# The border between two layers: weights laid out transposed, low parts moved to GpSimd, the first tile quantised earlier

## The reference

```
# layer 0: attention with context, 32 query heads, 8 kv heads, rotary, then a quantised gated FFN
x = x + tanh(g_xattn[0]) * (softmax(rope(LN(x) @ wq) @ rope(ctx @ wk).T / sqrt(128) + mask) @ (ctx @ wv)) @ wo
h = silu(q8(LN(x)) @ q4(Wg).T) * (q8(LN(x)) @ q4(Wu).T)        # q8: rows to 8 bits, q4: weights to 4 bits
x = x + tanh(g_ffn[0]) * (q8(h) @ q4(Wd).T)
# layer 1: attention over the channel axis, per sequence; then a linear layer with routed low-rank parts
q = Wq @ ctx' + bq ; k = Wk @ ctx' + bk ; v = Wv @ LN(x)' + bv  # Wq, Wk, Wv are 64x64, ctx' is [64, 512]
x = x + tanh(g_xattn[1]) * (v @ softmax(q.T @ k).T)
alpha = softmax(router_W[active] @ LN(x) + router_b[active] + log(domain_prior[active]))
x = x + tanh(g_ffn[1]) * (LN(x) @ W_base.T + b_base + 2 * sum_e alpha_e * (LN(x) @ A_e.T) @ B_e.T)
```

## Time and profile before

| | |
|---|---|
| time, median of 3 runs (lowest to highest) | 795.31 us (793.71 to 796.48) |
| the profiled execution | 795.32 us, span from first to last instruction 793.5 us |
| TensorE busy | 780.8 us, 98% of the span, 4940 instructions |
| TensorE weight loads | 638.8 us, 81% |
| VectorE busy | 541.4 us, 68% |
| ScalarE busy | 437.7 us, 55% |
| GpSimd busy | 498.0 us, 63% |
| granted TensorE clock | 1.000 in all slices |
| DMA | 71.02 MB in 77778 packets, 51552 of them under 512 B |

### The profile page before, as it was taken

How to read it: one execution, slowest core, us unless ns; L and a number is a source line. 1 busy time by engine, 2 the same in 40 slices (tenths; PEclk the granted TensorE clock), 3 DMA queues, 4 the chain that set the end, 5 groups by cost and what they waited for, 6 DMA issues and landing times.

```text
span 793.5 us, 13550 instructions
## 1 busy us (share of the span) xinstructions
PE 780.8 (98%) x4940; PEld 638.8 (81%) x4957; DVE 541.4 (68%) x1043; ACT 437.7 (55%) x824; POOL 498.0 (63%) x430
## 2 busy tenths in 40 slices
PE   8999999999999999999999999999999999999998
PEld 7888888888888888888888888888765777777776
DVE  6857866666676545466655555555899987998874
ACT  5754455444454434444454433333579898888773
POOL 2797477645556764475676456546457885887753
PEclk9999999999999999999999999999999999999999
DMA  9312533432523131952113111267273413213101
GB/s 335 107 66 68 139 80 81 133 97 72 148 77 89 40 102 58 47 147 77 63 40 105 43 51 27 36 64 277 82 191 95 107 48 81 74 49 80 48 16 40
DMA packets 77778, 71.02 MB, mean 89 GB/s; under 512 B 51552, under 2 KB 52800, under 8 KB 77328
## 3 DMA queue, kind: packets, MB, share of 16 engines
q1 hardware_dynamic: 77424, 69.82, 34.1%
q10 hardware_dynamic: 288, 0.33, 0.1%
HBM read 49.04 MB, written 6.34 MB: 70 GB/s over the span
## 4 chain that ended last, share of the span: by engine, by line
PE 87%; DVE 4%; DMA 4%; POOL 2%; ACT 2%; issue 1%; another core or an unknown queue 1%; SPq 0%; DVEq 0%
PE bank L81 11%; PE bank L83 10%; PE bank L82 10%; PE bank L554 7%; PE bank L577 6%; PE bank L572 6%; PE bank L573 6%; PE bank L667 4%; PE bank L1645 4%; PE bank L1631 3%; PE bank L1597 2%; PE bank L1568 2%; PE bank L1576 2%; PE bank L1621 2%; DMA w_out<-w_quant 2%; PE bank L1622 2%
## 5 line engine op out<-in xcount | busy, mean ns | idle before, releaser
L970 DVE SCALAR_TENSOR_TENSOR x_res<-bank,gate,x_res 128x512 f32<-128x512 f32 x128 | 95.4, 747 | 74.0 <-PE bank L577 73.4
L1231 POOL TENSOR_TENSOR prob<-prob,row_inv 128x512 f32<-128x512 f32 x32 | 33.4, 1044 | 166.1 <-DVE row_inv L966 159.5
L1217 POOL TENSOR_TENSOR rope_swap<-rope_swap,trig 128x512 f32<-128x512 f32 x80 | 104.0, 1300 | 30.6 <-ACT rope_swap L737 30.3
L736 ACT COPY rope_swap<-bank 64x512 f32<-64x512 f32 x80 | 46.7, 584 | 110.3 <-DVE rope_cos L941 110.2
L941 DVE TENSOR_TENSOR rope_cos<-bank,trig 128x512 f32<-128x512 f32 x80 | 54.2, 678 | 76.5 <-PE bank L83 71.4
L572 PE MATMUL bank<-wo_hi,oT_hi 128*128 128x512 f32 x256 | 101.7, 397 | 1.2 <-DVE x_res L970 0.6
L81 PE MATMUL bank<-xnT_hi,wq_hi 128*128 128x512 f32 x252 | 101.5, 403 | 0.0
L573 PE MATMUL bank<-wo_lo,oT_hi 128*128 128x512 f32 x256 | 100.8, 394 | 0.0
L83 PE MATMUL bank<-xnT_hi,wq_lo 128*128 128x512 f32 x252 | 99.9, 396 | 0.0
L82 PE MATMUL bank<-xnT_lo,wq_hi 128*128 128x512 f32 x252 | 99.5, 395 | 0.0
L1223 POOL TENSOR_TENSOR q_rope<-rope_cos,rope_swap 128x512 f32<-128x512 f32 x64 | 84.2, 1315 | 5.0
(11 more groups left out here) (273 smaller groups left out, 1936.2 us busy)
## 6 DMA issues: line engine op xcount, KB each, us to landing
wq_raw<-in_wq_tiles SPq DMA_DIRECT2D x16, 512.0 KB, 3.8
wo_raw<-in_L_xattn_wo SPq DMA_DIRECT2D x16, 512.0 KB, 3.9
xn<-in_L_ffn_Wd SPq DMA_DIRECT2D x16, 256.0 KB, 3.6
b_ctx<-in_ctx SPq DMA_DIRECT2D x32, 128.0 KB, 2.6
b_k_twice<-b_qk_hi SPq DMA_DIRECT2D x32, 128.0 KB, 2.4
w_T_dram<-w_out SPq DMA_DIRECT2D x28, 128.0 KB, 3.1
w_T<-w_T_dram SPq DMA_DIRECT2D x2, 1376.0 KB, 19.9
xn<-in_L_ffn_Wg SPq DMA_DIRECT2D x10, 256.0 KB, 3.0
```

Of the source, the lines that this page charges most:

```text
L970: dve.scalar_tensor_tensor(out=K.x[:, t, :], in0=wo_ps[t % 2][:, :], scalar=K.gate[:, 0:1], in1=K.x[:, t, :], op0=ALU.mult, op1=ALU.add).t ...
L1217: pool.tensor_tensor(out=sw, in0=sw, in1=sin_b, op=ALU.mult).then_inc(s_rope, 1)
```

## The change

The host lays out W_base, [Wq Wk], Wv (block diagonal) and lora_B transposed, as four more inputs, and the kernel loads them so. `qkv_T`, `base_T`, `b_T` and `bT_copy` are gone: ScalarE casts the high parts from SBUF, and the low parts of W_base are taken by GpSimd instead of VectorE. The first projections move from behind the last output product's tile 0 into slot 30, and write to the banks `proj` instead of `av`. `low_T` moves to slot 31 and writes to `score`; its last product is `logit_T` of its own. `gated_rows` moves from slot 31 to slot 29 on VectorE. GpSimd's iotas and clearing of `qk_w_lo` move into slot 29, its low parts of the context and its clearing of `k_lo` into slot 30. On VectorE `first_front` now comes ahead of the sum of tile 0 of the last unit. In TensorE's second list tiles 1 and 2 of the output product come ahead of `x_transpose(0)`, and `logits(0, 0)` and `low_b_select` ahead of `gate_mm(0, 0)`. SP waits for the last attention product instead of the clearings. Some buffers change places (`qk_lo` with `result`, `k_lo` with `q_stack`), which adds the wait of `first_lo_qk` on `s_w_lo`.

```diff
             sp.wait_ge(M.s_k_zero, 4)
+            sp.wait_ge(s_av, 2 * NPAIR)
...
-            def qkv_T():
-                pe.wait_ge(s_proj_read, len(ALL))
-                pe.wait_ge(R1.s_in, 16 * R1.n_loads)
-                for i in range(3):
-                    mm = pe.transpose(proj[0][0:S, i * S:(i + 1) * S], R1.qkv[i][:, :], K.ident[0:S, 0:S])
-                mm.then_inc(s_w_ps, 1)
...
-            def base_T(c):
-                if c == 1:
...
-                for o in range(DC):
-                    mm = pe.transpose(base_ps[c][:, o * P:(o + 1) * P], R1.base[:, o, c * P:(c + 1) * P], K.ident[:, :])
-                mm.then_inc(s_w_ps, 1)
...
             def low_T(cs):
...
-                    pe.wait_ge(s_sel, 11)
+                    pe.wait_ge(s_sel, 9)
+                    pe.wait_ge(s_soft, 5 * (2 * NPAIR - 1) + 1)
...
-                pe.matmul(trans[:, HD:HD + E_ACT], M.spread[:, :], M.sel_e[:, :], start=True, stop=True).then_inc(s_w_lowT, 1)
...
-            def b_T():
...
-                for c in range(DC):
-                    mm = pe.transpose(proj[0][:, c * P:(c + 1) * P], R1.b[:, c, :], K.ident[:, :])
...
+            def logit_T():
+                pe.wait_ge(s_sel, 11)
+                pe.matmul(score[:, HD:HD + E_ACT], M.spread[:, :], M.sel_e[:, :], start=True, stop=True).then_inc(s_w_lowT, 1)
...
             def low_b_select():
-                pe.wait_ge(s_w_lo, 4)
-                pe.wait_ge(s_w_bT_sb, 1)
-                pe.matmul(proj[1][:, :], M.sel[:, :, :].rearrange("p a n -> p (a n)"), M.bT[:, :], start=True, stop=True
+                pe.wait_ge(M.s_qk_lo[1], 1)
...
             def first_qk(par):
...
-                    pe.wait_ge(s_w_qkv, 4)
+                    pe.wait_ge(s_w_qkv, 1)
...
-                    pe.wait_ge(s_oT_lo, 2 * 2 * NPAIR)
+                    pe.wait_ge(s_proj_read, len(ALL))
...
                 if U == 2 * NPAIR - 1:
-                    base_T(1)
-                    base_T(2)
...
                 if U == 2 * NPAIR - 2:
-                    qkv_T()
-                    base_T(0)
+                    first_qk(0)
+                    first_qk(1)
+                if U == 2 * NPAIR - 1:
+                    low_T((2, 3))
...
             run_slots(slot)
-            base_T(3)
...
             def qkv_weights():
...
+                act.wait_ge(R1.s_in, 16 * R1.n_loads)
+                act.wait_ge(s_zero, 3)
+                act.copy(M.qk_w_hi[:, :], R1.qk[:, :]).then_inc(s_w_qkv, 1)
+                act.copy(M.v_w[:, :], R1.v[:, :]).then_inc(s_w_qkv, 1)
...
             def base_high_part(c):
-                act.wait_ge(s_w_ps, W_BASE + c)
...
+                part = BASE_ORDER[c]
+                act.copy(M.base_hi[:, part, :], R1.base[:, part, :]).then_inc(s_w_hi, 1)
...
-                    if U == 2 * NPAIR - 1:
+                    if U == 2 * NPAIR - 2:
+                        first_split_hi(1)
                         base_high_part(1)
+                        base_high_part(2)
...
+                    if U == 2 * NPAIR - 3:
+                        qkv_weights()
+                        first_split_hi(0)
+                        base_high_part(0)
                     if U == 2 * NPAIR - 2:
-                        qkv_weights()
-                        base_high_part(0)
-                        first_split_hi(0)
-                        first_split_hi(1)
+                        first_hi_qk(0)
+                        first_hi_qk(1)
+                        base_high_part(3)
                         prior_logarithm()
...
+            low_part()
...
             def first_lo_qk(par):
                 dve.wait_ge(M.s_qk_hi[par], 1)
...
+                dve.wait_ge(s_w_lo, par + 1)
...
             def gated_rows():
                 dve.wait_ge(K.s_gate, 1)
+                dve.wait_ge(R1.s_in, 16 * R1.n_loads)
                 dve.tensor_scalar(K.W1.base_row[:, :], K.W1.base_row[:, :], K.gate[:, 3:4], None, ALU.mult).then_inc(M.s_w_logit, 1)
                 dve.tensor_tensor(out=K.W1.bv[:, :], in0=K.W1.bv[:, :], in1=K.gate[:, 1:2], op=ALU.mult).then_inc(M.s_w_logit, 1)
...
                     selection_matrices()
+                    qk_w_low_part()
                 if U < 2 * NPAIR - 1:
                     soft_first(U + 1)
                 else:
                     statistics_end()
-                    base_low_part(1)
-                    gated_rows()
+                    first_lo_qk(0)
                     router_offset()
                 dve.wait_ge(s_oT_hi, 2 * U + 2)
...
                     soft_sum(U + 1)
-                if U == 2 * NPAIR - 2:
-                    qk_w_low_part()
-                    base_low_part(0)
+                if U == 2 * NPAIR - 3:
+                    gated_rows()
...
-            base_low_part(2)
             last = UT * (2 * NPAIR - 1)
...
                 front_tile(dve, M, 0)
+                accumulate(last, UT)
...
+                pool.wait_ge(s_w_hi, c + 1)
+                part = BASE_ORDER[c]
+                pool.tensor_tensor(out=M.base_lo[:, part, :], in0=R1.base[:, part, :], in1=f32(M.base_hi[:, part, :]), op=ALU.subtract
+                                   ).then_inc(s_w_lo, 1)
...
-                        pool.memset(M.v_w[:, :], 0.0).then_inc(s_zero, 1)
+                        pool.wait_ge(s_rope, 2 * rope_of(HKV - 1, len(ITEMS[-1])))
+                        pool.wait_ge(s_sel, 9)
+                        first_split_lo(0)
+                        first_split_lo(1)
+                        pool.wait_ge(M.s_ctx_lo[1], 1)
+                        base_low_part(0)
+                        pool.wait_ge(s_score, 2 * NPAIR)
+                        for i in range(2):
+                            for par in range(2):
+                                pool.memset(f32(M.k_lo[i][par][:, :]), 0.0).then_inc(M.s_k_zero, 1)
                     if U < 2 * NPAIR - 1:
                         normalise(U + 1)
                     for k, (G, pos) in enumerate(items):
...
                             wo_piece(2 * g + jp + 1, u)
+                        if U == 2 * NPAIR - 3 and k == 0:
+                            pool.wait_ge(s_wo_lo[1], NQP * (NPAIR // 2))
+                            pool.iota(M.rank_i[:, :], pattern=[[1, RANK]], base=0, channel_multiplier=0).then_inc(s_zero, 1)
+                            pool.iota(M.part_i[:, :], pattern=[[0, 1]], base=0, channel_multiplier=1).then_inc(s_zero, 1)
+                            pool.memset(f32(M.qk_w_lo[:, :]), 0.0).then_inc(s_zero, 1)
...
+            for c in range(1, DC):
+                base_low_part(c)
             pool.wait_ge(s_x_stat, 2 * UT + 1)
             pool.tensor_tensor(out=K.rstd[:, 0:UT], in0=K.var_eps[:, 0:UT], in1=K.minus_half[:, 0:UT], op=ALU.pow
                                ).then_inc(s_x_stat, 1)
...
         load(W.bv[h * S:(h + 1) * S, :], a["L1_xattn_bv"].unsqueeze(1))
-    for c in range(DC):
-        load(R.b[:, c, :].rearrange("p (e r) -> p e r", e=E_ALL),
-             a["L1_ffn_lora_B"][:, c * P:(c + 1) * P, :].rearrange("e p r -> p e r"))
-    for i, name in enumerate(("L1_xattn_Wq", "L1_xattn_Wk", "L1_xattn_Wv")):
-        load(R.qkv[i][:, :], a[name])
+    load(R.b[:, :], a["lora_b_T"])
+    load(R.qk[:, :], a["qk_T"])
+    load(R.v[:, :], a["v_T"])
...
 def load_base(sp, R, a):
-    sp.dma_start(R.base[:, :, :], a["L1_ffn_W_base"].rearrange("(c p) h -> p c h", p=P)).then_inc(R.s_in, 16)
+    sp.dma_start(R.base[:, :, :], a["base_T"]).then_inc(R.s_in, 16)
...
-    M.qk_lo, M.result = two("b_qk_lo", [P, D], F32R), two("b_result", [P, D])
+    M.result, M.qk_lo = two("b_result", [P, D]), two("b_qk_lo", [P, D], F32R)
...
-    M.q_stack, M.k_lo, M.k_twice = ([two(f"b_{n}{i}", [P, D], F32R) for i in range(2)] for n in ("q_stack", "k_lo", "k_twice"))
+    M.k_lo, M.q_stack, M.k_twice = ([two(f"b_{n}{i}", [P, D], F32R) for i in range(2)] for n in ("k_lo", "q_stack", "k_twice"))
...
                 if t == 0:
-                    pe.wait_ge(L0.s_w_lo, 3)
+                    pe.wait_ge(M.s_w_low, 1)
...
                 pe.matmul(sum_ps(t)[:, :], zT[:, :], low_b[:, :], start=False, stop=True).then_inc(s_y, 1)
-            first.qk(0)
-            first.qk(1)
-            first.low_T((0, 1))
+            first.logit_T()
             first.output(2 * NPAIR - 1, 1)
+            first.output(2 * NPAIR - 1, 2)
             x_transpose(0)
-            first.output(2 * NPAIR - 1, 2)
-            pe.wait_ge(s_qk_lo[0], 1)
+            logits(0, 0)
+            first.low_b_select()
             gate_mm(0, 0)
-            pe.wait_ge(s_qk_lo[1], 1)
             up_mm(0, 0)
-            first.low_b_select()
             pe.wait_ge(s_xT_sb, 1)
             qk(1, 0)
             first.output(2 * NPAIR - 1, 3)
-            logits(0, 0)
             pe.wait_ge(s_gate, 1)
             gate_mm(0, 1)
...
             pe.wait_ge(s_gate, 2)
             gate_mm(0, 2)
-            first.low_T((2, 3))
             logits(0, 3)
```

(4 more changed lines are left out.)

115 lines of the change are left out of this document (38 added, 77 removed).

## The result

Over 22 executions of each on the same chip the changed kernel takes 797.77 us (median; 795.45 to 802.67) and the kernel before 795.27 us (793.58 to 797.45): a ratio of 1.0032, interval 1.0022 to 1.0043, so slower by about 0.3%. The forecast was 795.8 us in a range up to 797.6 us, so the median lies 0.17 us outside. The profiled execution took 798.41 us. Of the 22 executions, four ran at a mean granted clock of 1.000 and took 795.45, 795.66, 796.5 and 797.25 us; the other eighteen ran at 0.993 to 0.998 and took 796.99 us or more (median 797.95).

The account below looks back on a forecast made before the run. TensorE, busy 780.8 of 793.5 us, was taken as the bound, with VectorE limiting between 580 and 602 us. Delays and savings summed to +0.5 us: span 794.0 us, plus 1.8 us gives 795.8 us, range 792.6 to 797.6.

Parts of the forecast that it names:

- Last scores: Slots 29 and 30: gated_rows (0.46 us) and short GpSimd instructions (0.4 us) delay the last attention scores from 557.05 to 557.9.
- the iotas: Slot 29: three short GpSimd instructions behind one wait, ahead of the last rotation, taken at 0.4 us (bounds 0.2 and 0.6).
- its rival at 0.09: Slot 30: VectorE's subtraction of the maxima and GpSimd's new instructions hold each other, giving 797.0 us; chance 0.09.
- the sum: Whole span: gains and delays added up to +0.5 us, 793.5 to 794.0 us.
- The 1.96 us copy: Slot 31, VectorE's 16x128 copy beside GpSimd clearings: shortened by moving them, its 0.67 us wait goes, but net -0.2 us.
- the step staked on: First tile: logits(0, 0), now ahead of gate_mm, wait for the fifth DMA copy until 579.1; TensorE idles 1.6 us.
- VectorE's chain: From scale_gate(0, 0) to 601 us: starts 1.0 us late, two gaps take up 0.45, leaving +0.5 us.
- The wait for the hidden layer: TensorE's 0.84 us wait at 602.41 grows, as four selections (1.2 to 1.4 us) at 587.94 are gone.
- The work taken away counts in full: Rival: copies in time and the 1.4 us at 587.94 passes through; 2.9 us gained, 792.4 us; chance 0.15.
- copies in time: Rival, at the first logits: no wait at 577.5, gate_mm starts at 578.7; about 1.0 us gained, 794.3 us; chance 0.16.
- Copies are late: Rival: slow landing and drawn-out issues put logits(0, 0) at 581.3; +2.7 us, 798.0 us; chance 0.10.

Follow-up runs that it names:

- e1: Changed kernel with the two instructions of gated_rows exchanged (128x1 product first, 128x512 scaling second); median 796.88 us, ratio 1.0014 to the kernel before.
- e4: Kernel before with only gated_rows moved to slot 29, including the changed kernel's wait for their loads; median 797.47 us, ratio 1.0018 to the kernel before.
- e6: Changed kernel unedited, timed again; median 797.13 us, ratio 1.0027 to the kernel before.
- e8: Changed kernel with TensorE's old order at the first tile (gate and up products ahead of the logits), rows still early; 796.76 us, ratio 1.0017 to the kernel before.
- e9: e5 with GpSimd's iotas and clearing behind the last rotation and ScalarE's query and key weight copies a slot later; 797.42 us, ratio 0.9981 to the kernel before.
- e11: e5 with TensorE's transposes of the first quantised tile ahead of output tile 2; median 797.87 us, ratio 0.9985 to the kernel before.
- e13: e11 with wide products placed between TensorE's narrow low-rank products around the last attention product; median 794.60 us, ratio 0.9974 to the kernel before.
- e7: Changed kernel with unused identity transposes on TensorE, 14 ahead of the last scores and ten ahead of the first logits' wait; 796.33 us, ratio 1.0013 to the kernel before.
- e2: Changed kernel with gated_rows back in slot 31, behind first_lo_qk(0); median 796.50 us, ratio 1.0010 to the kernel before.
- e5: Changed kernel with gated_rows back in slot 31 and TensorE's old order at the first tile (logits late); median 794.65 us, ratio 0.9994 to the kernel before.

## Why the prediction was wrong

**Last scores: the step that failed.** "gated_rows on VectorE ahead of the first times_cos (0.48 us alone, 0.46 us to the next start)". The price was read from slot 31, where GpSimd took the power of 128x4 elements while the two instructions ran (L1293, 570.31 to 571.33 in the kernel before), and the product beside it lasted 0.15 us. In slot 29 the product of two SBUF operands meets GpSimd's division and lasts as long: 1.29 us instead of 0.46. With the iotas' 0.43 us (taken at 0.4) the scores come 10.42 - 8.65 = 1.77 us late instead of 0.86. The prediction had the rule at hand, "SBUF — State Buffer", section "Who interferes with whom" of the Trainium skill, by which a VectorE instruction with two SBUF inputs and a GpSimd one that reads SBUF exclude each other; it applied the section to the copy that got faster, and its rival at 0.09 had a collision of this kind, but in slot 30 and for another subtraction: the right mechanism in the wrong place. e1 and e4 agree with it: 0.12 us when begun ahead of the division, 1.00 us when begun behind its start. That the 128x4 power, which reads SBUF too, didn't hold the product is a case that the rule as told here doesn't cover; why is open.

**The granted clock: not in the sum at all.** The prediction read 1.000 on the page and let TensorE idle for 0.86 and 1.6 us at no other price than the wait. The change makes two gaps and packs the narrow products together, and the clock fell in 18 of 22 executions and 10 of 12 of e6, but in 5 of the 69 of the kernel before beside e1 to e8 (14 of 29 beside e9 to e11, 2 of 17 beside e13). That is 1.15 and 2.27 us in the two profiles of the changed kernel; of the 2.5 us that the median rose, this part is not settled.

**What held.** At full clock the stretch grows by 1.01 us where the sum had 0.5, and it splits, by the profiles, into +1.18 (rows early, e7 less e2), +0.68 (logits early, e5 less e2) and -0.85 us (all the rest, e5 less the kernel before), from one profile each. So the work taken from TensorE did bring something, hidden by two of the moves. The 1.96 us copy shrank to 0.21. The logits do wait for the fifth copy, the step staked on, but 0.71 us and not 1.6 (0.68 in e2, at full clock): the loads took 2.39 us and not 3.1, and from the last attention product to the logits TensorE needed 0.36 us more than forecast. The 1.92 us of e1 came with a landing of 3.6 us. The 2.0 us of the Trainium skill that the prediction sets beside its row stands in a section on transfers issued by GpSimd; these copies are SP's, and the row's 2.4 us was right. VectorE's chain has no gap up to the maximum and takes up 0.72 us of the delay (0.45 forecast). The wait for the hidden layer, forecast to grow, didn't (0.83 us against 0.84); TensorE waits 0.34, 0.80 and 0.32 us between 587 and 595 us instead. "The work taken away counts in full" and "copies in time" didn't happen. "Copies are late" has the right size of result, 798.0 us, by luck: in the changed kernel they weren't late.

**What stays open.** Why the clock falls in some executions of a kernel and not in others, and why behind 1.89 us of idle time in one profile and not behind 1.96 us in another; what the narrow place contributes by itself; why e2's median is 0.89 us over the kernel before when its stretch is 0.17 us shorter.

## What to carry to other kernels

Before moving an instruction to another slot, list what the other engines run there: a price read from one neighbourhood (0.46 us) doesn't hold in the next (1.29 us), and the other order of two small instructions took 0.84 us of the shift away (e1). In a kernel in which TensorE is busy 98% of the time, a new gap can cost more through the granted clock than through the wait (2.27 against 1.01 us here), so compare several executions' clocks, look in the windows where the clock fell before blaming an edit, and fill a gap that can't be closed. Where the run-to-run scatter is as large as the effect, measure between two marks in the trace: 50.43, 49.58 and 48.87 us tell apart what the medians don't.

## What the runs showed of the hardware that was not expected

- An instruction of 128x1 elements lasted 1.00 us because GpSimd's 128x512 division had started 0.21 us earlier; started ahead of it, 0.12 us. The order of issue decided. A second one in the changed kernel, VectorE's scaling of 128x4 at 557.43, lasted 1.06 us beside GpSimd's rotation of 557.17, and 0.17 us in the kernel before. Beside GpSimd's 128x4 power the same product took 0.15 us.
- The granted clock fell to 1.2 GHz behind an idle 1.68 us (1.20 us in e4), and at the narrow place with TensorE busy for 2.00 of every 2.00 us around it. Behind an idle 1.96 us in e7 it didn't fall.
- With fourteen transposes (1.69 us) in the idle time the clock stayed at 2.4 GHz at the scores in the profiles of both kernels that had them; in the three with the same wait and no transposes (the changed kernel, e6, e8) it fell. They didn't delay the scores: 10.43 and 10.42 us after the reciprocal, 10.42 without them.
